# Layer 0 of a two-layer kernel: where the operands of the first two batches are made, and how they are stored

## The reference

```
xn = layernorm(x)
x1 = x + (xn + window_attention(xn)) + quantised_ffn(xn)
```

## Time and profile before

| | |
|---|---|
| median of 3 runs | 729.73 us (728.58 to 729.93) |
| the profiled execution | 732.44 us, span 730.4 us |
| busy, TensorE / VectorE / ScalarE / GpSimd | 575.6 / 465.4 / 341.5 / 316.1 us |
| opening, to the first scores of the loop | 0 to 63.8 us |
| first row maximum on VectorE | 43.66 us |
| batches of layer 0 in the loop | about 42 us each, to about 430 us |

### The profile page before, as it was taken

How to read it: one execution, slowest core, us unless ns; L and a number is a source line. 1 busy time by engine, 2 the same in 40 slices (tenths; PEclk the granted TensorE clock), 3 DMA queues, 4 the chain that set the end, 5 groups by cost and what they waited for, 6 DMA issues and landing times. The chain is left out here.

```text
span 730.4 us, 18096 instructions
## 1 busy us (share of the span) xinstructions
PE 575.6 (79%) x5741; PEld 360.6 (49%) x5742; DVE 465.4 (64%) x1896; ACT 341.5 (47%) x1037; POOL 316.1 (43%) x361
## 2 busy tenths in 40 slices
PE   2378887888888978889799849988972699999930
PEld 0135554555554545555465426666542366666620
DVE  3688767686777776766777037888875254445425
ACT  2202563654645646447466635655641244444410
POOL 6950533443332435423100014788874155555530
PEclk9999999999999999999999989999987699999975
DMA  2845036171381542702600223111211122222209
GB/s 58 176 99 103 31 81 125 31 162 46 74 160 32 119 87 59 169 25 69 136 18 18 75 77 149 57 58 45 71 54 49 34 74 76 73 76 73 76 15 345
DMA packets 51140, 61.18 MB, mean 84 GB/s; under 512 B 9841, under 2 KB 41973, under 8 KB 49280
## 3 DMA queue, kind: packets, MB, share of 16 engines
q1 hardware_dynamic: 45568, 49.73, 29.2%
q0 software_dynamic: 4352, 8.47, 3.5%
q10 hardware_dynamic: 1152, 2.10, 0.7%
HBM read 32.08 MB, written 28.45 MB: 83 GB/s over the span
## 5 line engine op out<-in xcount | busy, mean ns | idle before, releaser
L571 DVE CUSTOM_DVE_ANT_0 A<-A,band 128x320 f32<-128x320 f32 (+2 forms) x512 | 213.7, 467 | 92.6 <-PE A L729 91.7
L464 ACT ACTIVATE Pb<-SB 128x320 f32<-128x320 f32 (+2 forms) x512 | 176.2, 403 | 162.2 <-PE SB L759 159.0
L729 PE MATMUL A<-Ks,Qs 48*64 48x320 bf16 (+2 forms) x1024 | 151.3, 303 | 10.9 <-DVE mneg L571 9.7
L750 PE MATMUL SB<-Qs,Ks 50*64 50x320 bf16 (+2 forms) x1024 | 145.9, 290 | 3.6 <-ACT Pb L464 2.9
L759 PE MATMUL SB<-ends,ident 64*64 64x64 bf16 (+1 forms) x1024 | 106.7, 206 | 0.0
L1518 POOL DMA_INDIRECT results<-y,xt x72 | 70.7, 982 | 71.5 <-issue 37.6
L750 PEld LDWEIGHTS SB<-Qs,Ks 50*64 50x64 bf16 x1024 | 57.0, 107 | 58.5 <-issue 29.5
L729 PEld LDWEIGHTS A<-Ks,Qs 48*64 48x64 bf16 x1024 | 57.6, 110 | 48.5 <-DVE mneg L571 36.1
L1622 PE MATMUL UP<-w_up,xT 128*128 x144 | 80.1, 639 | 1.7 <-ACT xT L1531 1.2
L770 PE MATMUL PV<-Pb,Va 128*32 128x320 f32 (+2 forms) x1024 | 77.2, 422 | 0.0
L1080 POOL DMA_INDIRECT expert_rows<-pay,pos x64 | 62.9, 983 | 24.0 <-issue 17.8
(11 more groups left out here) (194 smaller groups left out, 973.4 us busy)
## 6 DMA issues: line engine op xcount, KB each, us to landing
Qs<-parts_dram SPq DMA_DIRECT2D x16, 384.0 KB, 6.1
Ks<-parts_dram SPq DMA_DIRECT2D x16, 384.0 KB, 8.9
xt<-expert_rows SPq DMA_DIRECT2D x72, 65.0 KB, 1.8
yb<-results SPq DMA_DIRECT2D x8, 512.0 KB, 6.8
parts_dram<-qp SPq DMA_DIRECT2D x16, 192.0 KB, 2.8
parts_dram<-kp SPq DMA_DIRECT2D x16, 192.0 KB, 2.8
l_xb<-x_dram SPq DMA_DIRECT2D x9, 256.0 KB, 3.0
xb<-in_x SPq DMA_DIRECT2D x8, 256.0 KB, 3.0
```

What stands on the lines that cost most here:

```text
L464: act.activation(Pb[:, group % 4, c, 0:w], SB[k % NB_BANKS][:, 0:w], ACT.Exp).then_inc(act_exp, 1)
L571: nc.vector.tensor_tensor_reduce(scores_of, scores_of, band[:, skip:skip + w], -1.0, 3e38, ALU.add, ALU.min, mneg[:, step % 2, col:col + 1 ...
L729: mm = nc.tensor.matmul(A[k % NA_BANKS][r0:r0 + HP, 0:w], Qs[b % RING][rows, a, HP * sub:HP * sub + HP], Ks[b % RING][rows, a, lo:lo + w], ...
L750: nc.tensor.matmul(out[r0:r0 + HP, 0:w], Ks[b % RING][rows, a, HP * sub:HP * sub + HP], Qs[b % RING][rows, a, lo:lo + w], start=True, stop ...
```

## The change

- **Batch 0's and 1's norm** (`norm`) go from GpSimd to VectorE; `normed(g)` gives the semaphore to wait for. Later batches keep it on GpSimd.
- **Banks.** For batch 0 q, k, values and ffn go to the banks SB[0], SB[1], SB[2] and again SB[1]; batch 1's q goes to PV. The rest stays in `misc`. The projections no longer wait for each other's evacuations.
- **K of batch 0** gets both its evacuations and all three terms on VectorE (`first_k`); q's stay on ScalarE and GpSimd. GpSimd's order has the clip ahead of q's terms and the conversion to xq (`quant_int`) behind them.
- **Stores.** `parts_dram` has the half (q, of 2) inside the term, so a store covers 128 partitions and an operand has three stores, not six, in every batch. The loads read the same amount, with a stride between the six terms.
- **Memsets.** Va's two stand first on VectorE; each Ks gets one memset over all partitions and not two over 32, one early and two just ahead of the maxima, with the two casts of the masks `ends16` behind them.
- **WARM.** 60 matmuls of 128x128x128 in bf16 into A[0] stand first on TensorE; nothing reads them.
- The first scores, and the first `attend`, wait for what last used their banks.

```diff
-    parts_dram = nc.dram_tensor("parts_dram", [NB, 2, 2, NTERM, HP, T], BF16).ap()
+    parts_dram = nc.dram_tensor("parts_dram", [NB, 2, NTERM, 2, HP, T], BF16).ap()
...
+    def normed(g):
+        return (dve_xn, NT * (g + 1)) if g < 2 else (pool_xn, NT * (g - 1))
...
+    def q_bank(g):
+        return (SB[0], PV, misc)[min(g, 2)]
+    def k_bank(g):
+        return SB[1] if g == 0 else misc
+    def v_bank(g):
+        return SB[2] if g == 0 else misc
+    def ffn_bank(g):
+        return SB[1] if g == 0 else misc
...
         def store_parts(g, which):
             tile, runs, done, ready = ((qp, QRUNS, dma_pq, pool_q3), (kp, KRUNS, dma_pk, pool_k3))[which]
-            sp.wait_ge(ready, g + 1)
-            for par in range(2):
-                for n, count, part, width in runs:
-                    src = tile[HP * par:HP * par + HP, part:part + width, :]
-                    if width < count:
-                        src = src.to_broadcast([HP, count, T])
-                    sp.dma_start(parts_dram[g, which, par, n:n + count].rearrange("n r t -> r n t"), src)\
-                        .then_inc(done, 16)
+            if which == 1 and g == 0:
+                sp.wait_ge(dve_k, 5)
+            else:
+                sp.wait_ge(ready, g + 1 - which)
+            for n, count, part, width in runs:
+                src = tile[:, part:part + width, :]
+                if width < count:
+                    src = src.to_broadcast([P, count, T])
+                sp.dma_start(parts_dram[g, which, n:n + count].rearrange("n q r t -> (q r) n t"), src)\
+                    .then_inc(done, 16)
...
-                                 parts_dram[g, which, par].rearrange("n (d a) t -> (n d) (a t)", a=NA))\
+                                 parts_dram[g, which, :, par].rearrange("n (d a) t -> n d (a t)", a=NA))\
...
-        sp.wait_ge(dve_fill, 2)
+        sp.wait_ge(dve_fill, 1)
...
-        sp.wait_ge(dve_fill, 2 * RING)
+        sp.wait_ge(dve_fill, RING)
...
         def base_x(g):
-            pool.wait_ge(pool_xn, NT * (g + 1))
+            pool.wait_ge(*normed(g))
             if g > 0:
                 pool.wait_ge(pool_b1, g)
...
         rstd_of(0)
-        norm(0)
         base_x(0)
         quant_scale(0)
-        for which in range(2):
-            rest(0, which)
-            second(0, which)
-            third(0, which)
+        quant_clip(0)
+        rest(0, 0)
+        second(0, 0)
+        third(0, 0)
         rstd_of(1)
-        norm(1)
-        quant_clip(0)
         quant_int(0)
-        pool.wait_ge(dve_const, 2)
+        pool.wait_ge(dve_const, 4)
         base_bias(0)
...
                 act.wait_ge(pool_rq, g)
-            act.activation(qf[:], misc[:], ACT.Identity, bias=bq_col[:, 0:1], scale=SC).then_inc(act_qf, 1)
...
-            if g > 0:
-                act.wait_ge(pool_rk, g)
+            if g == 1:
+                act.wait_ge(dve_k, 3)
+            else:
+                act.wait_ge(pool_rk, g - 1)
...
         def evac_k1(g):
-            if g > 0:
-                act.wait_ge(dma_pk, PARTS * g)
...
             act.wait_ge(pe_ctxT, g + 1)
             act.activation(ctxT[:], misc[:], ACT.Copy).then_inc(act_ctxT, 1)
-        for g in range(2):
-            evac_xnT(g)
-            evac_q(g)
-            evac_q1(g)
-            evac_k(g)
-            evac_k1(g)
+        evac_xnT(0)
+        evac_q(0)
+        evac_q1(0)
+        evac_xnT(1)
         evac_xqT(0)
+        evac_q(1)
+        evac_q1(1)
+        evac_k(1)
+        evac_k1(1)
         evac_mT(0)
...
+        def norm(g):
+            dve.wait_ge(pool_rs, g + 1)
+            if g > 0:
+                dve.wait_ge(pe_xnT, g)
+                dve.wait_ge(pool_t1, NT * g)
+                dve.wait_ge(pool_b0, g)
+                dve.wait_ge(dve_amax, g)
+            for i in range(NT):
+                nc.vector.tensor_scalar(xn[:, i, :], xb[:, i, :], mv[:, i, 0:1], rstd[:, i:i + 1],
+                                        ALU.subtract, ALU.mult).then_inc(dve_xn, 1)
+        def first_k():
+            dve.wait_ge(pe_k, 1)
+            nc.vector.tensor_scalar(kf[:], SB[1][:], b_col[:, 1:2], None, ALU.add).then_inc(dve_k, 1)
+            nc.vector.tensor_scalar(kp[:, 0, :], SB[1][:], b_col[:, 1:2], None, ALU.add).then_inc(dve_k, 1)
+            dve.wait_ge(dve_k, 2)
+            nc.vector.tensor_tensor(rk[:], kf[:], kp[:, 0, :], ALU.subtract).then_inc(dve_k, 1)
+            dve.wait_ge(dve_k, 3)
+            nc.vector.tensor_copy(kp[:, 1, :], rk[:]).then_inc(dve_k, 1)
+            dve.wait_ge(dve_k, 4)
+            nc.vector.tensor_tensor(kp[:, 2, :], rk[:], kp[:, 1, :], ALU.subtract).then_inc(dve_k, 1)
...
         def fill(i):
-            for par in range(2):
-                r0 = HP * par + 32
-                nc.vector.memset(Ks[i][r0:r0 + 32].bitcast(F32), ONE_PAIR).then_inc(dve_fill, 1)
+            nc.vector.memset(Ks[i][:].bitcast(F32), ONE_PAIR).then_inc(dve_fill, 1)
+        for i in range(2):
+            nc.vector.memset(Va[i][:], 0.0).then_inc(dve_const, 1)
         for i in range(NT):
             bn(0, i)
         ag(0)
+        norm(0)
         absmax(0)
         scales(0)
         dve.wait_ge(dma_rows, 16 * 6)
         nc.vector.tensor_copy(wq[:], wq8[:].bitcast(mybir.dt.int8)).then_inc(dve_const, 1)
         nc.vector.tensor_tensor(bsum_row[:], bo_row[:], fb_row[:], ALU.add).then_inc(dve_const, 1)
-        dve.wait_ge(pool_const, 10)
-        nc.vector.tensor_copy(ends16[:, 0, :], band[:, 0:HP]).then_inc(dve_const, 1)
-        nc.vector.tensor_copy(ends16[:, 1, :], band[:, 4 * HP:5 * HP]).then_inc(dve_const, 1)
+        fill(0)
         for i in range(NT):
             bn(1, i)
         ag(1)
-        for i in range(RING):
-            fill(i)
-        for i in range(2):
-            nc.vector.memset(Va[i][:], 0.0).then_inc(dve_const, 1)
-        dve.wait_ge(dve_const, 6)
+        first_k()
+        norm(1)
+        dve.wait_ge(dve_const, 2)
         for par in range(2):
             rows, col = slice(HP * par, HP * par + HP), 2 * HD * par + HD
             for i in range(2):
                 nc.vector.memset(Va[i][rows, :, :, col:col + 1], 1.0).then_inc(dve_const, 1)
+        evac_v(0)
+        absmax(1)
         for i in range(NT):
             ffn_out(0, i)
-        evac_v(0)
-        absmax(1)
         scales(1)
+        for i in range(1, RING):
+            fill(i)
+        dve.wait_ge(pool_const, 10)
+        nc.vector.tensor_copy(ends16[:, 0, :], band[:, 0:HP]).then_inc(dve_const, 1)
+        nc.vector.tensor_copy(ends16[:, 1, :], band[:, 4 * HP:5 * HP]).then_inc(dve_const, 1)
         for n in range(UNITS):
             maxima(0, n)
...
             pe.wait_ge(*before)
-            for i in range(NT):
-                mm = nc.tensor.transpose(misc16[:, i * P:(i + 1) * P], xq[:, i, :], ident16[:])
+            out = SB[0][:, 0:256].bitcast(BF16) if g == 0 else misc16
+            for i in range(NT):
+                mm = nc.tensor.transpose(out[:, i * P:(i + 1) * P], xq[:, i, :], ident16[:])
...
-                mm = nc.tensor.matmul(misc[:, i * P:(i + 1) * P], xqT[:, i * P:(i + 1) * P], wq[:],
+                mm = nc.tensor.matmul(ffn_bank(g)[:, i * P:(i + 1) * P], xqT[:, i * P:(i + 1) * P], wq[:],
...
+            if k == 0:
+                pe.wait_ge(act_xqT, 1)
+                pe.wait_ge(dve_ffn, NT)
+                pe.wait_ge(dve_v, 4)
+                pe.wait_ge(dve_const, 10)
...
+            if sub == 0 and step == 0:
+                pe.wait_ge(act_q1, 2)
...
         pe.wait_ge(pool_const, 6)
-        turn_xn(0, (pool_xn, NT))
+        for i in range(WARM):
+            nc.tensor.matmul(A[0][:, 0:P], ident16[:], ident16[:], start=True, stop=True)
+        turn_xn(0, normed(0))
         pe.wait_ge(dma_w, 32)
         project(0, 0, pe_q, (act_xnT, 1))
-        project(0, 1, pe_k, (act_q1, 1))
-        turn_xn(1, (act_k1, 1))
+        project(0, 1, pe_k, (act_xnT, 1))
+        values(0, (act_xnT, 1))
+        turn_xn(1, (act_xnT, 1))
+        pe.wait_ge(act_q1, 1)
+        turn_xq(0, (act_q1, 1))
         project(1, 0, pe_q, (act_xnT, 2))
-        project(1, 1, pe_k, (act_q1, 2))
-        turn_xq(0, (act_k1, 2))
+        project(1, 1, pe_k, (act_xnT, 2))
         pe.wait_ge(dve_const, 4)
+        pe.wait_ge(dve_k, 2)
         ffn_mm(0, (act_xqT, 1))
-        values(0, (dve_ffn, NT))
         for n in range(UNITS):
             piece(0, n)
-        turn_max(0, (dve_v, 4))
+        turn_max(0, (act_k1, 1))
```

More of the change, by code:

```diff
@@ L51 @@
 NB_BANKS = 3
+WARM = 60
 def reach(s):
@@ L299, in norm @@
             pool.wait_ge(pool_rs, g + 1)
-            if g > 0:
-                pool.wait_ge(pe_xnT, g)
-                pool.wait_ge(dve_amax, g)
-                pool.wait_ge(pool_t1, NT * g)
-                pool.wait_ge(pool_b0, g)
+            pool.wait_ge(pe_xnT, g)
+            pool.wait_ge(dve_amax, g)
+            pool.wait_ge(pool_t1, NT * g)
+            pool.wait_ge(pool_b0, g)
             for i in range(NT):
```

(19 more changed lines are left out.)

22 lines of the change are left out of this document (10 added, 12 removed).

## The result

| | before | after |
|---|---|---|
| median of the runs | 729.83 us (4 runs, 728.58 to 732.56) | 748.85 us (4 runs, 744.50 to 752.16) |
| ratio, 95% interval | | 1.025 [1.019, 1.031] |
| span of the profiled execution | 730.4 us | 747.1 us |
| first row maximum on VectorE | 43.66 us | 37.74 us |
| first scores of the loop | 63.82 us | 57.89 us |

The forecast was 721.2 us, in a range of 717 to 725. The kernel became 19 us slower. The opening did become shorter, by 5.9 us of the 8.5 forecast; the loop of layer 0 (first scores to last evacuation of PV) went from 361.51 to 382.55 us, 21.0 us more; the rest of the kernel, from `l_bqs` on, took 298.2 us after and 297.9 before.

What follows compares the result with a forecast made beforehand. The opening was taken to bound the gain, the loop only passing it on. With data at 33.8 and VectorE last at 35.1, the first maximum moves from 43.66, saving 8.5 us: 729.73 - 8.5 = 721.2 us, range 717 to 725.

Steps and rivals of the forecast that it cites:

- 2. norm of batch 0 on VectorE: Opening: batch 0's norm takes 1.12 us on VectorE against 3.13 on GpSimd, ending at 8.65 instead of 9.69.
- 5. three stores: Opening: about 0.66 us per store, 2.0 us for three; q from 17.2 to 19.2, k to 21.2 or up to 23.
- 7. VectorE ready for the first maximum: Opening: batch 1's norm starts in effect at 20.8, then 14.3 us of work put the first maximum at 35.1.
- 8. sixty matmuls: Start of TensorE: they lie under x's load and the statistics; no effect taken, bounds 0 to 2 us of delay.
- Step 6: Opening: Q's loads issued at 21.9, all data landed 11.9 us later, at 33.8; with slow stores 35.8.
- the loop's paragraph: Loop: batch 2's last load has 1.6 us to spare, the queue is about 2 us quicker; hidden, worth nothing.
- Slower: the new layout's load: Rival: strided loads spread worse over the DMA engines, costing opening and batches 2 to 7; 742 us at y = 6; chance 0.06.
- y: Microseconds a batch by which the new loads spread worse over the DMA engines, in the slower rival.
- the formula: Slower rival: y + 6 (y - 3.6) = 8.5, opening plus six batches' loss against the gain; decides at y = 4.3.
- data becomes the limit: Rival, opening: late K passes or stores no faster than 201 GB/s; data at 36 to 37.5, 723 us; chance 0.14.
- TensorE did become fast at the start: Rival, opening: sixty matmuls bring the 2.4 GHz level and it holds to 28 us; gain 9.9 us, 719.9; chance 0.14.
- step 3: Opening, GpSimd: the clip, ending at 13.85, just fits under q's projection and evacuation; q's terms ready at 17.2.

Runs made afterwards that it cites:

- e3: Changed kernel with each load reading 48 rows that follow one another in DRAM, so attention uses other operands; 720.70 us, 0.989 of the kernel before.
- e1: Changed kernel with the old layout, its six stores and its loads put back; 725.11 us, 0.994 of the kernel before.
- e4: e1 without the sixty matmuls at the start; 725.79 us, 0.995 of the kernel before.
- e5: Changed kernel with a head's eight rows outermost in the loads and the terms inside; 754.17 us on chip 2, 0.990 of the kernel before there.
- e7: e1 with the second half of batch 0's stores issued by ScalarE; 751.34 us on chip 2, 0.988 of the kernel before there.
- e8: e5 with SyncE waiting for batch 0's loads before the next x load and batch 1's stores; 752.82 us on chip 3, 0.987 of the kernel before.
- e10: The same kernel as e5, run again on chip 3; 756.02 us, 0.990 of the kernel before there.
- e6: Changed kernel with each load cut in two of three terms; 827.26 us on chip 2, 1.086 of the kernel before there.

## Why the prediction was wrong

| step | forecast | measured in the changed kernel |
|---|---|---|
| 2. norm of batch 0 on VectorE | 1.12 us, ends 8.65 | 1.12, ends 8.87 |
| 3. q's terms ready | 17.2 | 17.55 |
| 5. three stores, q / both issued by | 2.0 us / 21.2 to 23 | 1.59 us / 21.46 |
| 6. Q's loads issued | 21.9 | 21.57 |
| 6. data, from that issue | 11.9 us (33.8) | 15.8 us (37.33); on sixteen engines 13.3 (34.83, e3) |
| 7. batch 1's norm, start in effect (end less 1.12 us) | 20.8 | 20.1 |
| 7. VectorE ready for the first maximum | 35.1 | 34.04 |
| first maximum to first scores | 20.2 us | 20.15 us |
| 8. sixty matmuls | 0 | 0.25 us on q's terms, nothing in the median (e1 against e4) |
| loop | as before, loads with 1.6 + 2 us to spare | 21.0 us longer, seven waits |

**Step 6 failed, and the loop's paragraph with it.** The step took 11.9 us for the loads "from Q's issue", carried over from a load that reads 48 uniform rows to one that reads six blocks of eight. It was treated as the same transfer: its bytes, its rows and its direction are the same. The row that would have asked the question is the share in the kernel before: 1.02 of sixteen engines, with 170 GB/s, while loads alone ran. The loads filled all the engines, so how many the new pattern would fill had to be asked, and never was. Six were too few; eight, as e5 shows, are enough.

The Trainium skill (DMA: Bandwidth & Descriptors, Why a DMA increments its semaphore by 16 and not by 1) states how many engines a DMA uses: the largest number up to 16 that divides the slowest dimension, of those larger than 1, of both access patterns. For 48 rows on both sides that is 16, for 6 x 8 against 48 partitions 6, for 8 x 6 it is 8, and for 3 x 8 against 24 it is 3. Shares of 1.02, 0.39, 0.50 and 0.19 in these runs agree in all four. The same page's rules advise an outermost dimension that is a multiple of 16.

**The rival had the place right, and its price and chance wrong.** "Slower: the new layout's load" named the mechanism, the opening's loss and the margin in the loop. Three things in it fell:
- "Against: each block is still 8 rows of 1 KB, as before" is no argument. (Nor is the figure right: a block is 8 rows of 8 KB.) What an engine gets is not decided by the size of a block but by how many blocks the outermost dimension has. On that sentence alone the chance was 0.06.
- In the opening y was 15.8 - 11.9 = 3.9 us, or 2.5 against the 13.3 us of e3. By the formula either is below the deciding 4.3 and would have left the kernel faster. The opening did come out ahead, by 5.9.
- In the loop y is not one number. It was 3.8 in batch 2, just over the margin of 3.6 (3.2 as measured: TensorE was ready 15.9 us after the issue, 12.7 being the time that the loads took before), with a wait of 0.57 us; but the loads of batch 3 took 20.5 us and TensorE waited 5.44. The formula gives 6 x (3.8 - 3.6) = 1.2 us for the loop, and it lost 21.0: the loads of batch 3 took longer, their last engines finished late (share 0.13), and matmuls ran at the lower clock for longer behind the long waits. A margin from one batch was taken as the margin of six; a seventh, batch 1, was left out, whose loads go out at 53.11 and for which TensorE waited 0.77 us at 70.72.

**Where it was right.** The steps of the opening up to the issue of the loads hold within 0.4 us, the tail of 20.2 us is rigid in every run, and e3 shows that the sum is right under the forecast's own assumption. That is partly luck, for it hides an error of size in each of two terms: with all sixteen engines data came 13.3 us after the issue in e3, not 11.9 (12.0, 12.6 and 13.3 in e4, e7 and e1), and VectorE is ready at 32.8 in e3 (35.24 - 2.45) and 34.04 in the changed kernel, not at 35.1. So it is the rival "data becomes the limit" that holds in e3, e5 and e8, by 1 to 3 us of idle VectorE, at a time that happens to be the forecast's. The issue of stores was forecast rightly as a price for each instruction, whatever it carries (0.53 to 0.75 us for 128 partitions, 0.66 for 64), and e1 shows what it was worth: 4 us of 8.4 in the first maximum (3 by e4, which has six stores too).

**VectorE and GpSimd held each other up more often than charged, and the norm less.** The norm of batch 1 took 1.70 us instead of 1.12 beside the conversion of xq, 0.6 more where 1.5 was charged. GpSimd's third term of q took 1.47 instead of 1.16 beside VectorE's conversion of K's rest (1.26), and its rstd 1.45 instead of 1.04. Together 1.3 us beyond those rows' durations; the path that ended last, the loads, carries 0.3 of it (q's third term, ahead of the first store).

**TensorE did become fast at the start.** The rival's first half is true (1.95 us for both projections of batch 0); its second half is not: batch 1's projection of q, after 8 us in which TensorE stood idle and then transposes, took 2.04 us again, and the first rate bought 0.25 us (e4): the clip covers the rest, as step 3 said it would.

**What stays open.** Why the loads of batches 3 to 6 take longer from the issue of Q's to the piece (20.5, 19.1, 18.6 and 18.1 us) than those of batches 2 and 7 (16.5 and 16.9), and why two of six engines finished 5 us late in batch 3: in both kernels a store and a load of `base` are queued right behind them, and no run took those away. How the 5.7 us of the loop beyond the waits divide. Whether e8's wait is a gain. Why eight engines load as fast as sixteen here: a packet of 8 KB takes about 0.35 us on eight (e5, 56 to 60 us) and 0.78 on sixteen (62 to 66 us of the kernel before), but no run shows what they then wait for.

## What to carry to other kernels

Before changing the layout of a tensor in DRAM, write down for each transfer that touches it the outermost dimension of both patterns, after the change as well as before: a pattern that used to merge into 48 rows and now reads 6 x 8 leaves ten of sixteen engines idle, and swapping two dimensions of the same load took the ratio from 1.025 to 0.990 here (on different chips, each against its own kernel before). Where loads run alone and are queued ahead, multiply the DMA share by 16 and read it as a number of engines; the 0.87 of the old stores is no such number, since a doubled store raised it to 1.01 and the rate by two thirds. A load whose share is near 1 is one to ask about before a change that lowers it, though half the engines were enough here. A transfer with a small margin in one batch is to be followed through all of them, since one that is just late in the second was 5 us late in the third.

## What the runs showed of the hardware that had not been expected

- A load of 48 partitions moved 79 GB/s on three engines, 133 on six, 180 to 201 on eight and 170 to 174 on sixteen: about 22 to 26 GB/s an engine up to eight, and then no more. The time from the issue of Q's loads to the first piece was 24.7 us on three, 15.8 on six, 13.1 to 13.8 in three runs on eight and 12.0 to 13.3 in four on sixteen.
- Stores of 128 partitions instead of 64 moved 340 GB/s instead of 201, with the engines busy 1.01 and 0.87.
- Beside loads on few engines the queue takes longer to issue the next transfers: batch 1's three stores of q occupied SyncE for 1.58 us beside loads on sixteen engines (e3), 1.78 and 2.06 on eight (e10, e5), 4.37 on six and 13.48 on three (e6, with twice as many loads). The loads of batch 0 were still in flight when these stores were issued; that this is the cause is not tested.
- The granted clock in the records is 1.00 for the opening of the kernel before and 0.50 for much of that of the changed one, while the same projection took 2.05 and 2.04 us. So the mean clocks of the two kernels (0.942 and 0.890) can't be compared; durations can.
